# Differential attention over 32 short sequences: stationary values in column groups, 32-row score tiles, the row norm folded in, and a longer pipe

## The reference

```python
# tokens: 32 x 36 patches of 768 numbers
y = layernorm(patches, g1, b1) @ Wp + bp; h = concat([layernorm(y, g2, b2), txt], axis=1)
# differential attention: 8 heads, 16 half heads of 16 columns, values 32 wide
n = layernorm(h)
q, k = rotary(rmsnorm(n @ Wq.T)), rotary(rmsnorm(n @ Wk.T)); v = n @ Wv.T
attn = softmax(causal(q @ k.T / sqrt(16)))            # 16 maps of 113 x 113
attn = attn[:, :, 0] - lam * attn[:, :, 1]            # 8 maps
h = h + (layernorm(attn @ v) * (1 - LAMBDA_INIT)) @ Wproj.T
# feed-forward with blockwise FP4 rounding of inputs, weights and hidden values
h = h + fp4_linear(silu(fp4_linear(layernorm(h), w_gate)) * fp4_linear(layernorm(h), w_up), w_down)
```

## Time and profile before

| | |
|---|---|
| median of 3 runs | 660.13 us (658.75 to 660.40) |
| the profiled execution, its own time | 662.52 us |
| its span, first to last instruction | 660.8 us |
| mean granted clock of TensorE | 0.948 |
| TensorE, VectorE busy | 576.4 us (87%), 554.1 us (84%) |
| ScalarE, GpSimd busy | 322.1 us (49%), 309.8 us (47%) |

### The profile page before, as it was taken

One profiled execution on the slowest core, in us unless ns is written; L12 is line 12 of the kernel. 1 busy time (PEld: TensorE's weight loads), 2 busy tenths in 40 slices (PEclk: granted clock), 3 DMA queues, 4 the chain that ended last, 5 costly groups with the idle time before them and its releaser, 6 DMA issues. The chain is left out here.

```text
span 660.8 us, 14226 instructions
## 1 busy us (share of the span) xinstructions
PE 576.4 (87%) x3666; PEld 470.0 (71%) x3666; DVE 554.1 (84%) x1444; ACT 322.1 (49%) x760; POOL 309.8 (47%) x455
## 2 busy tenths in 40 slices
PE   5665568999999999999999998589999999999996
PEld 4554455767776776777677676478888888888885
DVE  5999847898889889888988985498888888888884
ACT  2242215655665665566565564244544444445442
POOL 2455523555455445545554553155455445545542
PEclk9878776999999999999999997789999999999999
DMA  6900000011111111111111101111111111111111
GB/s 173 325 17 23 24 16 18 27 38 41 30 40 35 35 35 38 40 34 37 35 41 29 42 23 46 30 39 49 48 54 52 54 48 54 49 48 48 57 32 35
DMA packets 33734, 31.99 MB, mean 48 GB/s; under 512 B 6098, under 2 KB 32050, under 8 KB 33714
## 3 DMA queue, kind: packets, MB, share of 16 engines
q1 hardware_dynamic: 33714, 31.75, 16.3%
HBM read 23.02 MB, written 8.71 MB: 48 GB/s over the span
## 5 line engine op out<-in xcount | busy, mean ns | idle before, releaser
L741 PE MATMUL bank<-v_sb,pt 113*113 113x33 f32 x1024 | 109.1, 262 | 0.0
L741 PEld LDWEIGHTS bank<-v_sb,pt 113*113 113x113 f32 x1024 | 108.4, 181 | 0.7 <-issue 0.7
L858 POOL TENSOR_SCALAR_AFFINE_SELECT pt<-pt 113x452 f32<-113x452 f32 x128 | 73.9, 600 | 68.5 <-ACT pt L798 68.5
L798 ACT ACTIVATE pt<-bank 113x452 f32<-113x452 f32 x128 | 63.1, 545 | 38.2 <-PE bank L729 38.2
L138 PE MATMUL bank<-wgu_hi,fx_hi 128*128 128x512 f32 x174 | 69.5, 399 | 8.0 <-DVE fx_lo L1131 8.0
L1177 POOL TENSOR_TENSOR h_deq<-fh,fhb 128x704 f32<-128x704 f32 x29 | 40.3, 1389 | 68.8 <-DVE fhb L1084 56.3
L729 PE MATMUL bank<-q_blk,k_t 64*113 64x452 f32 x256 | 67.7, 605 | 0.0
L138 PE MATMUL bank<-wgu_hi,fx_lo 128*128 128x512 f32 x174 | 66.8, 384 | 0.0
L138 PE MATMUL bank<-wgu_lo,fx_hi 128*128 128x512 f32 x174 | 66.7, 384 | 0.0
L138 PE MATMUL bank<-wqkv_hi,xo_hi 128*113 128x256 f32 (+1 forms) x128 | 50.3, 393 | 17.7 <-DVE xo_lo L923 17.7
L1191 POOL TENSOR_TENSOR fh<-fh,fhb 128x704 f32<-128x704 f32 x29 | 40.3, 1391 | 42.2 <-DVE fhb L1145 42.2
(11 more groups left out here) (160 smaller groups left out, 1531.3 us busy)
## 6 DMA issues: line engine op xcount, KB each, us to landing
xb<-h_dram SPq DMA_DIRECT2D x29, 129.0 KB, 2.1
rb<-h_dram SPq DMA_DIRECT2D x29, 128.0 KB, 2.0
h_dram<-h SPq DMA_DIRECT2D x32, 112.9 KB
out<-res SPq DMA_DIRECT2D x28, 128.0 KB, 1.7
px<-in_patches SPq DMA_DIRECT2D x9, 384.0 KB, 10.1
hx<-in_txt SPq DMA_DIRECT2D x32, 77.0 KB
hr<-in_txt SPq DMA_DIRECT2D x32, 77.0 KB
wf<-in_wgu SPq DMA_DIRECT2D x1, 1408.0 KB, 8.0
```

The costliest lines, as they stand in the source:

```text
L741: mm = pe.matmul(pv_ps[s % 2][0:T, s // 2, :], pt[0:T, s, :], v_sb[0:T, s // 2, :], start=True, stop=True, skip_group_check=True)
L798: act.activation(pt[0:T, GS * g:GS * (g + 1), :].rearrange("p s t -> p (s t)"), sc_ps[g % 2][0:T, :], ACT.Exp, scale=1.0 / math.sqrt(HD)). ...
L858: pool.affine_select(out=grp, in_=grp, compare_op=ALU.is_ge, fill=0.0, base=0, pattern=[[0, GS], [1, T]], channel_multiplier=-1).then_inc( ...
```

## The change

The attention step is rewritten; the feed-forward part keeps its work, and the front has the attention weights prepared otherwise.

- *Values stationary.* pv becomes eight matmuls with the 32 value columns of a head stationary and 226 columns of exponentials (two maps) moving. Each writes 32 partitions of the output, so heads 0 to 3 and 4 to 7 stand in four column groups of TensorE. The output comes transposed: ScalarE copies it (ot_copy) and four transposes turn it back (pv_transposes).
- *Scores in 32-row tiles.* ROW is 32 instead of 64, so each of eight matmuls takes 32 rows, four row groups in four banks, and SLOTS is 2: q_blocks makes two copies.
- *Row norm in centred weights.* The columns of the attention weights are centred over the rows in the front, so hx is transposed as it is, without ln_apply. q and k need no scale but an epsilon times the row's variance (epsilons, on GpSimd, a 17th column of the squares); v gets the row's scale in v_stage.
- *Zero-sum value basis.* The values of a head are turned in the front into 31 columns whose norm is that of the centred values, and the 32nd column is a constant for the row sums. eps0, z_var and qk_var go.
- rope_sum moves to GpSimd, v_move goes, the low parts of the attention weights move from GpSimd to VectorE in the front.
- *Nine-step pipe* (b = -4 to 35), two sequences a loop iteration (6 to 27), with two buffers for the split inputs, the values and rstd.

```diff
-ROW = P // 2
+ROW = P // NG
...
+        OD, LD, ZD, UD = 5, 1, 3, 5
+        LOOP = (6, NSEQ - 4)
...
+            def load(s, _):
...
+                after(sp, m["ln_stats"], s)
+                after(sp, m["xo_made"], s)
+                load_rows(sp, hx, s, m["hx_loaded"])
...
+            def load_residual(s, _):
+                after(sp, m["h2_added"], s)
+                load_rows(sp, hr, s, m["hr_loaded"])
...
+            def steps(b, odd):
+                run_order(b, odd, one, ((-4, store), (-2, load_residual), (4, load)))
...
+            def transposes(s, odd):
+
+                after(pe, m["h2_added"], s - OD)
+                after(pe, m["xo_low"], s)
+                if one(s):
...
+                    pe.wait_ge(m["hx_loaded"], 32 * s + 32)
+                    for c in range(KD):
+                        mm = pe.transpose(xo_ps[:, c, :], hx[0:T, c * P:(c + 1) * P], ident[0:T, 0:T])
+                if one(s - OD):
+                    pe.wait_ge(m["o_made"], s - OD + 1)
+                    for c in range(KD):
+                        mm = pe.transpose(xo_ps[:, KD + c, :], o[0:T, c * P:(c + 1) * P], ident[0:T, 0:T])
                 mm.then_inc(m["xo_made"], 1)
...
+            def scores(s, odd):
...
+                pe.wait_ge(m["q_blocked"], s + 1)
+                pe.wait_ge(m["kt_copied"], s + 1)
+                after(pe, m["exp_made"], NG * s)
+                after(pe, m["ot_copied"], s)
+                for c in range(KD):
+                    for r in range(NG):
+                        rows = slice(r * ROW, (r + 1) * ROW)
+                        mm = pe.matmul(sc_ps[r][0:T, c * SLOTS * T:(c + 1) * SLOTS * T], k_t[rows, c, :],
+                                       q_blk[rows, c, :, :].rearrange("p s t -> p (s t)"),
+                                       start=True, stop=True, skip_group_check=True)
+                        if c == KD - 1:
+                            mm.then_inc(m["scores_made"], 1)
+
+            def pv(s, odd):
+
+                pe.wait_ge(m["masked"], NG * s + NG)
+                pe.wait_ge(m["v_staged"], s + 1)
+                for c in range(KD):
+                    for r in range(NG):
+                        mm = pe.matmul(ot_ps[r * VD:(r + 1) * VD, c, :, :].rearrange("p s t -> p (s t)"),
+                                       v_sb[odd][0:T, c * NG + r, :],
+                                       pt[0:T, r, c * SLOTS:(c + 1) * SLOTS, :].rearrange("p s t -> p (s t)"),
+                                       start=True, stop=True, skip_group_check=True)
                 mm.then_inc(m["pv_made"], 1)
...
+            def steps(b, odd):
+                run_order(b, odd, exists, (
+                    (-1, pv), (0, scores), (-1, pv_transposes), (-3, project), (2, qk), (3, transposes),
+                    (2, v), (1, qk_transposes)))
...
+            def steps(b, odd):
+                run_order(b, odd, exists, (
+                    (0, k_copy), (0, q_blocks), (-1, ot_copy), (1, v_stage), (0, exps, 0), (0, exps, 1),
+                    (0, exps, 2), (-1, z_square), (2, squares), (0, exps, 3), (3, xo_high), (2, roots)))
...
+            def steps(b, odd):
+                run_order(b, odd, some, (
+                    (-4, join_moments), (1, sines), (0, mask, 0), (0, mask, 1), (1, rope_sum), (0, mask, 2),
+                    (0, mask, 3), (3, epsilons)))
...
+            def steps(b, odd):
+                run_order(b, odd, exists, (
+                    (1, newton_step), (1, scale_qk), (3, ln_variance), (-2, o_apply), (1, cosines),
+                    (-1, ratios), (-1, mix_product), (-1, mix_sum), (-3, residual), (-3, out_sums),
+                    (-3, out_variance), (4, ln_sums), (2, qk_sums), (-1, z_sums), (3, xo_low)))
...
-            with engine.Fori(4, NSEQ - 3) as b:
-                attention(b)
+            with engine.Fori(LOOP[0], LOOP[1] - 1, step=2) as b:
+                attention(b, 0)
+                attention(b + 1, 1)
```

More of the change, by code:

```diff
@@ L768, in attention_tensor, with roots @@
+            exists = partial(some, joint=transposes)
             return steps
         def attention_scalar(act):
-            def roots(b):
-                act.wait_ge(m["variances"], b + 4)
-                if seq(b, 2):
-                    act.wait_ge(m["qk_var"], b + 3)
-                if seq(b, -1):
-                    act.wait_ge(m["z_var"], b)
+            def roots(s, odd):
+                after(act, m["newton"], 3 * (s + LD))
+                if one(s):
+                    act.wait_ge(m["qk_sums"], s + 1)
+                if one(s - ZD):
+                    act.wait_ge(m["z_sums"], s - ZD + 1)
+                if one(s + LD):
+                    act.wait_ge(m["ln_var"], s + LD + 1)
+                if one(s - UD):
+                    act.wait_ge(m["out_var"], s - UD + 1)
@@ new lines, in z_sums, with qk_sums, residual @@
+            def z_sums(s, odd):
+                dve.wait_ge(m["z_squared"], s + 1)
+                dve.tensor_reduce(var[0:T, HEADS], z2[0:T], AXX, ALU.add).then_inc(m["z_sums"], 1)
+            def qk_sums(s, odd):
+                dve.wait_ge(m["qk_squared"], s + 1)
+                dve.wait_ge(m["eps_set"], s + 1)
+                dve.tensor_reduce(var[0:T, QK], sq[0:T], AXX, ALU.add).then_inc(m["qk_sums"], 1)
+            def residual(s, odd):
+                dve.wait_ge(m["proj_made"], s + 1)
+                dve.wait_ge(m["hr_loaded"], 32 * s + 32)
+                after(dve, m["h2_stored"], 32 * s)
@@ L992, in steps, with out_variance @@
-            def steps(b, between=None):
-                run(b, seq, (
-                    ((2, -3), newton_step), (2, ln_apply), (-2, o_apply), (1, scale_qk), (1, cosines),
-                    ((2, -2), xo_low)))
-                if between:
-                    between()
-                run(b, seq, (
-                    (3, ln_sums), (-1, mix), (1, rope_sum), (-2, residual),
-                    (2, qk_sums), (-1, z_sums), (-2, out_sums), (-1, z_var), (2, qk_var),
-                    ((3, -2), variances)))
+            def out_variance(s, odd):
+                dve.wait_ge(m["out_stats"], 2 * s + 1)
+                pass_wait(dve, dve_passed)
+                dve.bn_aggr(moments[0:T, 1, :], st_out[0:T]).then_inc(m["out_stats"], 1)
+                dve.wait_ge(m["out_stats"], 2 * s + 2)
+                dve.tensor_scalar(var[0:T, 1:2], moments[0:T, 1, 1:2], LN_EPS, None, ALU.add).then_inc(m["out_var"], 1)
```

568 lines of the change are left out of this document (282 added, 286 removed).

## The result

The changed kernel takes 749.23 us, median of four runs (747.84 to 750.25), against 659.79 us for the kernel before on the same chip: a ratio of 1.136 (95% interval 1.133 to 1.138). The forecast was 738 us with a range of 680 to 775. It was right in sign and size, and the time of the likeliest case was 11 us short.

A forecast was written before the change was run, and what follows sets the result against it. VectorE was taken to set the old 9.60 us step; the change adds a wait for hx (10.7 us a step) and 1.4 us of lower clock, 12.1 us: 660.1 + 31 x 2.5 = 738 us, range 680 to 775.

The forecast's parts named there:

- the likeliest case: Attention loop: wait for hx plus lower clock, 12.1 us a step, 738 us in all; 50 in 100.
- The ends: Front and tail outside the attention loop: taken at zero change, with 8 us either way.
- Ring 1: Loop from TensorE's scores to transposes, SyncE's hx load, VectorE's sums, ScalarE's copies, back to scores: 10.74 us a step.
- The clock: TensorE idles some 4 us before scores, so its burst starts at 1.2 GHz: 1.4 us a step, at most 2.3.
- the fourth rival: TensorE's clock stays at the lower level through the whole burst: 15.2 us a step, 834 us; 6 in 100.
- Ring 2: Through VectorE: residual's end releases residual and hx loads, 3.6 us to data, ln_sums waits 2.7 us; steps 10.2 to 11.2.
- The lock: VectorE's o_apply and cosines wait out GpSimd's sines on the shared SBUF ports: 0 to 1.0 us, taken as 0.5.
- VectorE's own work: VectorE's work in each attention step without waits for others: 7.5 us, down from 9.02.
- Values in column groups: TensorE's eight value matmuls, 16 records: 0.95 us if four run together, 3.8 one by one; 0.95 taken.
- Mode changes: TensorE's tiling changes, three more a step: nothing added; 0.5 us at one 0.17 us tail each.
- The clock holds: Rival: TensorE's clock stays up in the loop, steps of 10.7 us, 694 us; 27 in 100.
- The load hides: Rival: new hx is there when VectorE asks, steps of 8.0 us including 0.5 for GpSimd, 611 us; 12 in 100.

The follow-up runs named there:

- the filler run: Changed kernel with 16 extra matmuls of 452 columns between values and scores each step, their result overwritten: 712.3 us, 1.080 of the kernel before.
- Experiment nine: Changed kernel, one hx buffer, ln_sums last in VectorE's step and o_apply ahead of scale_qk and cosines: 636.12 us, 0.959 of the kernel before.
- experiment two: Changed kernel with two hx buffers and SyncE's hx load ahead of the store and residual rows: 638.24 us, 0.966 of the kernel before.
- experiment seven: Changed kernel with two hx buffers, the load first in SyncE's step, and o_apply ahead of scale_qk and cosines: 629.63 us, 0.953 of the kernel before.
- experiment eight: Changed kernel with two hx buffers, load first, o_apply early, and 8 extra matmuls between values and scores: 627.18 us, 0.951 of the kernel before.
- experiment six: Changed kernel with only o_apply moved ahead of scale_qk and cosines in VectorE's order: 748.64 us, 1.133 of the kernel before.

## Why the prediction was right, and where its sizes were off

**The result by the forecast's terms.** It gave 31 steps x 2.5 = 78 us; the stretch measured 86.5. The ends were taken at zero with 8 us either way and are -6.9 and +6.5, so they cancel.

**Ring 1, forecast 10.74 us.** The order of work was right in each link. In the step shown, SyncE and landing take 2.64 us (forecast 2.76), VectorE 1.53 (1.39 and 0.04 to the root), ScalarE 2.12 (1.93), to TensorE 0.14 (0.12). TensorE at 2.4 GHz, from the filler run, takes 299.17 to 303.78 less 0.25 of wait = 4.36 (4.50), its scores 0.96 (1.2) in it. The sum is 10.79, put together from two runs.

**The clock, forecast 1.4 us.** This is the mis-sized term: 12.84 - 10.79 = 2.05 us in the mean, near the upper bound of 2.3. The trace says the same directly: from the scores' start to the transposes' end TensorE takes 5.6 to 7.1 us over the 21 steps of the loop, 6.5 in the mean, where 4.36 are its time at 2.4 GHz. The forecast chose 1.4 because the idle was at the short side of the earlier trace rows. It is 3.9 us long as predicted. In the step shown, TensorE's part is 7.03 for 4.36 us, 2.67 more and so above that bound: scores, back transposes, projection and nearly all of qk run slow, and only the norm's transposes are back at their old pace. That goes some way to the fourth rival, in which the whole burst stays at the lower level. The 1.4 was a choice between 0 and 2.3. The steps of the loop are 0.74 us longer than the 12.1 forecast, the ten around it shorter (11.65 in the mean), and all 31 take 386 us for 31 x 12.1 = 375: the 11 us that the likeliest case was short. As ring 2 is longer than ring 1 at 2.4 GHz, removing the cause gives back only 1.5 of the 2.05.

**Ring 2, forecast 10.2 to 11.2 us, taken as 10.7.** Measured 11.35 with the filler. The wait was 2.75 (2.7). The lock was 0.55 + 0.52 = 1.07 us, just above the upper end of "0 to 1.0", where I took 0.5: with cosines and o_apply behind scale_qk the sines get in first (299.28, ahead of o_apply's 299.32). (The Trainium skill, SBUF — State Buffer, section "SBUF: two separate sides", has the pair of ports held for a whole instruction by whoever starts first; the two orders agree, 0.97 against 0.42 us for the same o_apply.) "Both rings agree" was therefore wrong by half a microsecond, without effect on the kernel as it is, where ring 1 with its clock is longer.

**VectorE's own work, forecast 7.5 us.** Experiment nine shows it: 5.04 us from ln_sums to the residual's end and 2.50 from there to the end of xo_low (303.69), together 7.54.

**Values in column groups, forecast 0.95 us.** The 16 records take 0.97 (267.94): four groups run together.

**Mode changes.** I added nothing for them, on a misreading. In the earlier trace rows L138 starts behind a wait of 0.58 us for xo_low; what follows 64-row scores directly is L756, and scores follow L138. Nor are there three more changes: a step has three (to the values' tiles, to the scores' tiles, back to the full array), where it had four. Record by record the changes do show a little. Before, the last two projection records start 0.12 us apart, and the scores, which wait for nothing in the profile, start 0.21 behind the last (213.86):

```profile
213.53 0.28 PE L138 MATMUL bank_a<-wproj_lo,xo_hi 128*113 128x256 f32 x1
213.65 0.28 PE L138 MATMUL bank_a<-wproj_hi,xo_lo 128*113 128x256 f32 x1
```

In the filler run the rounds of four scores start 0.19 us apart, and the back transposes start 0.33 behind the last round (299.81 to 300.13). That is some 0.1 us at each of the two, and no run separates it from other causes of a late start. (The Trainium skill, TensorEngine Tiling (Array Packing), section "Key Properties", says that changing the tiling mode drains TensorE; these 0.1 us would agree.) In the sum it changes nothing, as the 0.96 us of the scores hold the one behind them.

**The rivals.** "The clock holds" (694 us) was made real by the filler and took 712. "The load hides" (611 us) was made real by experiments two and seven: 638 and 630, since VectorE's time beside GpSimd and the back transposes were more than its 0.5. What stays open is why some steps of experiment seven are 1.3 us longer than others; the filler of experiment eight made them even, at a mean step only 0.16 us shorter, and gave no clear gain.

## What to carry to other kernels

When a buffer's release moves from one engine to another, walk from the release over the issuing queue and the landing to the first reader, and then look at what stands behind that reader in its engine's order. Here the kernel with the late load is 89 us slower than the old one when the reader stands ahead of work that another engine waits for, and as fast as the old one when it stands last. Since the other edits are a gain, the load itself costs more than that: 111 us against experiment two, which hides it. With o_apply early it is 119 us (748.6 against seven's 629.6) with the reader ahead, and 6.5 (636.1) with it last. A second buffer by itself gave back 31 us, and the rest only when the queue's order let the load out. Add a ring's links again after every edit: a microsecond saved on an engine counts if the engine is in the ring, even while that engine shows a wait for a transfer (experiment nine), and not if a longer ring runs beside it (experiment six).

The version with two buffers, the load first and o_apply early takes 629.6 us, 0.953 of the kernel before. With one buffer and two changed entries in VectorE's order it is 636.1.

## What I had not expected

- A new wait of 1.2 us a step in the old kernel cost 0.33 us: by the trace it shifted VectorE off GpSimd's masks, whose cost (0.62 against 0.15 us for an instruction on eight numbers) shows in no list of waits.
- Sixteen filler matmuls a step made the changed kernel 37 us faster.
- A loop with TensorE's granted clock at 0.92 and steps of 8.5 to 9.5 us beats the old loop, which ran at 1.00 throughout. With TensorE in the ring the filler's full clock gave 37 us, and without the load's ring (eight against seven) nothing clear.
